# Gate and up products of an FP4 feed-forward regrouped into 512, 512 and 384 columns, with new instruction orders

## What is computed

```python
s = attn(xn)      # linear attention, 16 heads of 64, phi = elu + 1; + residual, LN; GELU FFN 256-1024-256; + residual, LN
gate = fp4_linear(xn, w_gate)               # 256 -> 704
y    = fp4_linear(xn, w_up)                 # 256 -> 704
g = silu(fp4_linear(silu(gate) * y, w_down))   # 704 -> 256
out = x + s * g
```

## Time and profile before

| | us |
|---|---|
| median of 3 runs | 1647.81 (1647.04 to 1648.1) |
| the profiled execution's own time | 1644.95 |
| its span in the trace | 1643.2 |
| PE busy, granted clock | 1604.9 (98%), 0.999 of full speed |
| DVE, ACT, POOL busy | 1280.4, 980.1, 783.3 |

### The profile page before, as it was taken

One profiled execution on the slowest core, in us unless ns is written; L12 is line 12 of the kernel. 1 busy time (PEld: TensorE's weight loads), 2 busy tenths in 40 slices (PEclk: granted clock), 3 DMA queues, 4 the chain that ended last, 5 costly groups with the idle time before them and its releaser, 6 DMA issues.

```text
span 1643.2 us, 30638 instructions
## 1 busy us (share of the span) xinstructions
PE 1604.9 (98%) x10977; PEld 1440.9 (88%) x10977; DVE 1280.4 (78%) x2485; ACT 980.1 (60%) x1770; POOL 783.3 (48%) x750
## 2 busy tenths in 40 slices
PE   7999999999899999999999999999999999999997
PEld 6878888888789998999999999989899989999897
DVE  6785664554788797888888887879788888878797
ACT  6665666655564747565665647474656656574743
POOL 4564543434242635444444536364455444363636
PEclk9999999999999999999999999999999999999999
DMA  7422323331501111133121112111121321111110
GB/s 227 136 84 86 104 78 106 103 109 57 186 15 53 52 53 52 53 111 91 47 68 53 52 53 107 53 52 53 52 60 61 104 87 58 53 52 53 52 53 26
DMA packets 92515, 123.46 MB, mean 75 GB/s; under 512 B 13503, under 2 KB 60747, under 8 KB 91342
## 3 DMA queue, kind: packets, MB, share of 16 engines
q1 hardware_dynamic: 92366, 121.51, 23.1%
HBM read 86.86 MB, written 34.62 MB: 74 GB/s over the span
## 4 chain that ended last, share of the span: by engine, by line
PE 68%; DVE 13%; DMA 7%; issue 5%; SPq 3%; ACT 3%; POOL 2%; DVEq 0%; POOLq 0%; ACTq 0%
PE QH L81 11%; PE QH L82 11%; PE QH L83 10%; PE AC L81 5%; PE AC L82 4%; PE AC L83 4%; DMA zb<-z_scratch 4%; PE GU L81 4%; PE GU L83 4%; PE GU L82 4%; DVE QH L1828 2%; PE TT L831 2%; DVE rl L1837 2%; SPq L408 2%; DMA z_scratch<-dn_s 1%
## 5 line engine op out<-in xcount | busy, mean ns | idle before, releaser
L2309 POOL TENSOR_TENSOR hb<-hb,rs_h 128x704 f32<-128x704 f32 x64 | 89.0, 1391 | 206.3 <-DVE rs_h L1680 206.3
L1248 ACT ACTIVATE hb<-GU 128x352 f32<-128x352 f32 x128 | 59.2, 463 | 214.3 <-PE GU L83 214.3
L1201 ACT ACTIVATE rh<-QH 128x512 fp32r<-128x512 f32 x256 | 151.2, 598 | 58.2 <-DVE QH L1828 53.2
L81 PE MATMUL GU<-wgh,xqh 128*128 128x352 f32 x512 | 169.8, 332 | 3.1 <-DVE hb L1673 3.1
L2315 POOL TENSOR_TENSOR hb<-hb,sn_h 128x64 f32<-128x64 f32 x64 | 18.8, 293 | 319.5 <-DVE hb L1685 319.5
L83 PE MATMUL GU<-wgh,xql 128*128 128x352 f32 x512 | 165.0, 322 | 0.0
L82 PE MATMUL GU<-wgl,xqh 128*128 128x352 f32 x512 | 164.9, 322 | 0.0
L1843 DVE TENSOR_TENSOR rl<-QH,rh 128x512 fp32r<-128x512 f32 x128 | 86.0, 682 | 85.8 <-ACT rh L1201 83.7
L81 PE MATMUL AC<-Mh,rh 128*128 128x256 f32 x512 | 145.9, 285 | 1.4 <-ACT rh L1201 0.6
L81 PE MATMUL AC<-w2h,rh 128*128 128x256 f32 x512 | 145.7, 285 | 0.0
L82 PE MATMUL AC<-Ml,rh 128*128 128x256 f32 x512 | 142.4, 278 | 0.0
(11 more groups left out here) (234 smaller groups left out, 5586.0 us busy)
## 6 DMA issues: line engine op xcount, KB each, us to landing
zb<-z_scratch SPq DMA_DIRECT2D x256, 128.0 KB, 3.0
xa<-in_L_attn_src SPq DMA_DIRECT2D x16, 512.0 KB, 4.2
xt_scratch<-xth SPq DMA_DIRECT2D x32, 256.0 KB, 2.7
xt_scratch<-xtl SPq DMA_DIRECT2D x32, 256.0 KB, 3.0
xb<-in_L_attn_src SPq DMA_DIRECT2D x16, 512.0 KB, 4.2
xnTh<-xt_scratch SPq DMA_DIRECT2D x32, 256.0 KB, 4.8
xnTl<-xt_scratch SPq DMA_DIRECT2D x32, 256.0 KB, 5.6
out<-x SPq DMA_DIRECT2D x15, 512.0 KB, 6.6
```

What stands on the lines that cost most here:

```text
L81: e.matmul(outp, lh, rh, start=start, stop=False, skip_group_check=check)
L1201: e.activation(RH[j % 4][:], src, ACT.Copy).then_inc(S[sem], 1)
L1248: e.activation(HB[i % 3][:, hf * HALF:(hf + 1) * HALF], gu_bank(i, hf)[:, 0:HALF], ACT.Tanh, scale=0.5).then_inc(S["th"], 1)
L2309: e.tensor_tensor(hb, hb, spread(rs_h[i % 2][:], 44), ALU.mult).then_inc(S["hin"], 1)
```

## The change

`gate_up(i, 0)` now makes 512 gate columns into the first bank of GU and 512 up columns into the second, 6 matmuls each, with a semaphore step after each part; `gate_up(i, 1)` makes the other 192 gate and 192 up columns together, as one run of 384 columns, 6 matmuls, into one bank (the first for even tiles, the second for odd). That is 18 matmuls a tile and 72 a group, in place of 24 and 96, over the same columns. The rows of the weights are loaded in the order that this needs. `gate_up(i, 0)` waits for each bank by itself; where the bank held a gate part only, it waits for hu, the first of DVE's two products. ACT and DVE have as many instructions as before, now of 512 and 192 columns.

Four dummy buffers move wgh, wgl and xqh, xql, Q32, eg, hb to 192 modulo 256 bytes and leave w2h, wdh and Mh at 224. All four engine lists are reordered.

```diff
-HALF = 352
+HEAD = 512
+SECTIONS = ((0, 512, 0, 0), (512, 512, 1, 0), (1024, 192, 0, 512), (1216, 192, 1, 512))
...
+GU_ORDER = ((0, 0), (0, 1), (1, 1), (1, 0), (2, 0), (2, 1), (3, 1), (3, 0))
+GU_ENDS = [sum(2 - hf for _, hf in GU_ORDER[:n + 1]) for n in range(8)]
...
+        sb("after_w2", [128, 56])
...
+        sb("after_wg", [128, 8])
...
+        sb("before_xq", [128, 8])
...
-        sb("before_m", [128, 32])
+        sb("before_m", [128, 24])
...
+        def gate_cols(i, hf):
+            return (GU[:, 0:512], HEAD) if hf == 0 else (GU[:, i % 2 * 512:i % 2 * 512 + 192], 704 - HEAD)
+        def up_cols(i, hf):
+            return GU[:, 512:1024] if hf == 0 else GU[:, i % 2 * 512 + 192:i % 2 * 512 + 384]
...
+                if hf:
+                    w.wait_ge(S["hu" if t % 2 == 0 else "hh"], n if t % 2 == 0 else n - 1)
+                    for kt in range(2):
+                        last = mm3(e, GU[:, t % 2 * 512:t % 2 * 512 + 384], xqh[:, kt, o:o + 128], xql[:, kt, o:o + 128],
+                                   wgh[:, kt, 1024:1408], wgl[:, kt, 1024:1408], kt == 0, kt == 1)
+                    last.then_inc(S["guG"], 1)
                 else:
+                    for up in range(2):
+                        if t % 2:
+                            w.wait_ge(S["hh"], n - 1 + up)
+                        else:
+                            w.wait_ge(S["hh" if up else "hu"], n)
+                        c = up * 512
+                        for kt in range(2):
+                            last = mm3(e, GU[:, c:c + 512], xqh[:, kt, o:o + 128], xql[:, kt, o:o + 128],
+                                       wgh[:, kt, c:c + 512], wgl[:, kt, c:c + 512], kt == 0, kt == 1)
+                        last.then_inc(S["guG"], 1)
```

More of the change, by code:

```diff
@@ L805, in gate_up @@
                 w.wait_ge(S["A_wTl"], 6)
[L806 to L809, removed]
-                else:
[L812 to L819, removed]
+                n = 8 * g + GU_ORDER.index((t, hf))
+                if hf:
[4 more added lines that the diff above has]
+                    last.then_inc(S["guG"], 1)
+                else:
+                    for up in range(2):
[8 more added lines that the diff above has]
+                        last.then_inc(S["guG"], 1)
             def turn_h(i, hf):
@@ L1026, in _ @@
+                turn_xq(g + 1, 0)
+                q_proj(g + 1, 6)
+                q_proj(g + 1, 7)
             f_step(NG - 2, 6)
             f_step(NG - 2, 7)
-            gate_up(NT - 3, 0)
+            den_sums(NG - 1)
+            gate_up(NT - 4, 0)
+            gate_up(NT - 4, 1)
+            gate_up(NT - 3, 1)
             down(NT - 6)
             turn_h(NT - 5, 0)
-            gate_up(NT - 3, 1)
-            turn_h(NT - 5, 1)
+            gate_up(NT - 3, 0)
             at_step(NG - 1, 0)
@@ L2034, in _ @@
             z_mul(0, 7)
[L2035 removed]
+            h_round(0)
             z_lo(0, 6)
             z_lo(0, 7)
[L2038 to L2039 removed]
+            gate_mul(1, 0)
+            xq_lo(0, 1)
             ln1_add(0, 0)
@@ L2107, in _ @@
                 z_mul(g, 3)
-                h_lo(d - 4, 1)
+                g_mul(c - 4)
                 z_lo(g, 2)
@@ L2112, in _ @@
                 z_mul(g, 5)
-                xq_lo(g, 1)
+                h_lo(d - 4, 1)
                 z_lo(g, 4)
@@ L2117, in _ @@
                 z_mul(g, 7)
-                gate_mul(b, 1)
+                h_round(a)
                 z_lo(g, 6)
                 z_lo(g, 7)
-                h_round(a)
-                g_mul(c - 4)
-                gate_mul(c, 1)
+                gate_mul(b, 0)
+                xq_lo(g, 1)
                 ln1_add(g, 0)
@@ L2174, in _ @@
                 q_elu(g + 1, 7)
-            x_round(NG - 1, 1)
-            gate_mul(NT - 4, 0)
-            den_inverse(NG - 1)
-            h_max(NT - 4)
-            h_scale(NT - 4)
-            ln_add("lnb", NG - 2, 0)
-            ln_add("lnb", NG - 2, 1)
-            ln_stats("lnb", NG - 2)
-            gate_mul(NT - 3, 0)
-            g_mul(NT - 6)
+                xq_lo(g + 1, 0)
+                ln_add("lnb", g, 0)
+                x_round(g + 1, 1)
+                den_inverse(g + 1)
+                ln_add("lnb", g, 1)
+                gate_mul(a + 4, 0)
+                ln_stats("lnb", g)
+            gate_mul(NT - 4, 1)
+            gate_mul(NT - 3, 1)
+            h_max(NT - 4)
             z_mul(NG - 1, 0)
@@ L2191, in _ @@
             z_mul(NG - 1, 3)
-            h_lo(NT - 5, 1)
+            g_mul(NT - 6)
             z_lo(NG - 1, 2)
@@ L2195, in _ @@
             z_mul(NG - 1, 4)
+            h_scale(NT - 4)
             z_mul(NG - 1, 5)
-            xq_lo(NG - 1, 1)
+            h_lo(NT - 5, 1)
             z_lo(NG - 1, 4)
```

609 lines of the change are left out of this document (332 added, 277 removed).

## The result

The changed kernel takes 1656.14 us in the median of 4 runs (1654.83 to 1656.72), the kernel before in the same comparison 1647.95 (1647.04 to 1648.32). The ratio is 1.0049 [1.0032, 1.0067], slower by 8.2 us. The forecast was 1642 with a range to 1655: the wrong sign, and outside. The profiled execution has a span of 1654.0 and an own time of 1655.8, 10.8 us more in span than the one before, which lay 2.9 us under its median.

What follows compares the result with a forecast made beforehand. It took PE's nearly gapless train of matmul calls, by product count and spacing, and its few stops as the bound. The terms -5.0 - 10.9 - 1.4 + 3.7 + 4.6 + 3.4 = -5.6 gave 1642 us, range 1630 to 1655.

Steps and rivals of the forecast that it cites:

- The stop that goes: PE's turn_h waiting behind h_lo, 8.7 us in 14 waits: expected to vanish, -10.9 us.
- D: In times such as D + 8.5, den_sums' end; as rival, 512-column products at the new place 8 ns slower, 1648, chance 0.05.
- at0's wait: PE's at0 right behind turn_h waits for z_lo0, 2.8 us in all; half taken as gone, -1.4 us.
- The products: Gate_up matmuls on PE: 0.227 us at 512 columns, 0.173 at 384, 0.078 less a tile, -5.0 us.
- The stops that come: Three new or longer waits on PE in the new order: +3.7, +4.6 and +3.4 us.
- (1): G(a,1) on PE waits for hu from G(a,0): 0.23 us, 16 times, +3.7 us.
- (2): turn_x1's second call on PE waits longer for ln1_norm: +0.3 us a group, 15 times, +4.6 us.
- (3): G(c,1) on PE waits for hu of (c,0), behind ln1_norm on DVE: 0.23 us, 15 times, +3.4 us.
- The other moves: Remaining reorderings, such as turn_xq, den_sums with f6 and f7 as cover, and the tail: costed at nothing.
- C: Rival: DVE's queue ahead of z_mul0, with den_inverse still late, makes it slower, 1657 or from 1651 up; chance 0.20.
- A: Rival: new order better balanced, the new stops hide and at0's whole wait goes, 1629; chance 0.15.
- B: Rival: stops only change places, products save 1 to 5 us, 1643 to 1647, say 1645.5; chance 0.24.

Runs made afterwards that it cites:

- e1: Changed kernel, but POOL's h_in(a) of a group's first tile waits until DVE has done h_lo(d',0); 1648.79 us, ratio 0.9996 to the kernel before.
- e6: Kernel before, with only h_scale(a) on VectorE and h_in(a + 4) on POOL moved to the changed kernel's places; 1664.04 us, ratio 1.008.
- e5: Changed kernel with h_lo(d - 4, 0) moved between z_mul(g, 0) and z_mul(g, 1) on VectorE; 1655.11 us, ratio 1.0032.
- e10: e9 with turn_h(d - 4, 0) also moved between G(a, 0) and G(a, 1) on PE; 1649.43 us, ratio 1.0003.
- e11: e3 with f_step(g - 1, 4) moved from ahead of q_proj(g, 4) to directly behind den_sums(g); 1658.39 us, ratio 1.0055.
- e3: Kernel before, products regrouped to 512, 512 and 384 columns, old orders and old buffer places; 1646.69 us, ratio 0.9979.
- e4: Whole changed kernel, but with the buffers at their old places; 1656.84 us, ratio 1.0046.
- e7: e3 with h_lo(d - 4, 0) moved between z_mul(g, 0) and z_mul(g, 1) on VectorE; 1651.16 us, ratio 1.0006.
- e9: e1 with turn_h(a, 1) moved between the two turn_x1 calls on PE; 1649.92 us, ratio 1.0006.
- e2: Kernel before, products regrouped to 512, 512 and 384 columns, old orders but new buffer places; 1647.91 us, ratio 0.9993.

## Why the prediction was wrong

**The stop that goes, -10.9: the step that failed.** The step said that h_lo would be 2.8 us less urgent and the stop would go "if the chain below holds". The chain held up to z_mul 0. It had den_inverse at D + 0.1 and z_mul 0 at D + 8.5; with D at 1120.61 they came at D + 0.2 and D + 8.3. Then the working took the pair z_mul 0 and 1 at the duration that it has alone, 1.3, and it took 2.47. The 12.6 us in 14 waits, each with 0.16 on top as in the forecast's own reading, cost 14.8 where 10.9 had been before: +3.9 in place of -10.9, which by itself turns -5.6 into +9. The working listed every instruction ahead of z_mul 0 on VectorE. It did not ask what the reciprocal, moved to directly ahead of z_mul 0, releases on POOL. e1 shows that this overlap is the cause of the loss, and e6 that it is enough by itself to make one. e5 adds that this stop could not have been had back at turn_h alone.

**Even without the collision the stop would have stayed in part.** e1 still has 4.5 us in 6 waits, and the DMA row in e10 says why. The path from den_sums over the denominators, the DMA and z_mul to h_lo and z_lo was already as long as PE's work beside it. More PE work behind turn_h's first half made h_lo less urgent against that half, but not against D, from which z_mul 0 and h_lo are counted. Before, PE was ready for turn_h(d',1) at D + 10.3 (1122.48 + 0.16); in the changed kernel it is ready at 1130.62 + 0.23, D + 10.2. The forecast's own numbers say the same: at0 at D + 10.6 less turn_h's 0.45 is D + 10.2, and h_lo's end is z_mul 0 at D + 8.5, the pair's 1.3 and h_lo's 0.4, again D + 10.2. That is a tie, so the -10.9 had no room behind it. This is a second error of the same step, and e1 fits it: without the overlap with z_mul 0 and 1 the kernel is back at the time before, and not 5.6 us under it. To get h_lo earlier, den_sums has to come earlier in PE's list, and e11 shows what stands against it.

**at0's wait, -1.4.** turn_h to at0 is 0.55 in starts, as it was: nothing gained. Off by 1.4.

**The products, -5.0.** Where no other width or transpose stands ahead the spacings are as forecast: G(d,0) of group 9 has 12 products in 2.72 us (1155.97 to 1158.69), 0.227 each, and the 384 settle at 0.173. But the first product behind a transpose or another width takes longer, 0.28 us at 384 columns (1123.67 to 1123.95 below), and the forecast had no such term. In G(a,0) and behind it group 9 has 512 columns at 0.230 (1122.10 to 1123.25 for five spacings), the 384 at 0.176 (1123.95 to 1125.71 for ten). That is 12 x 0.230 + 6 x 0.176 = 3.82 us a tile for 3.84 before, -1.5 us in all, below the 1.9 which the forecast had as the smaller end. The rows:

```profile
1122.10 0.40 PE L80 MATMUL GU<-wgh,xqh 128*128 128x512 f32 x1
...
1123.25 0.39 PE L82 MATMUL GU<-wgh,xql 128*128 128x512 f32 x1
1123.67 0.44 PE L80 MATMUL GU<-wgh,xqh 128*128 128x384 f32 x1
1123.95 0.33 PE L81 MATMUL GU<-wgl,xqh 128*128 128x384 f32 x1
...
1125.71 0.34 PE L82 MATMUL GU<-wgh,xql 128*128 128x384 f32 x1
```

The runs of e3 put the regrouping's whole worth in the old orders at 0.21% of 1649, 3.5 us; where the 2 us beyond the spacing come from was not followed up.

**The stops that come.** All three came, and a little smaller. (1) From the last 512 product at 1123.25 to the first 384 one at 1123.67 are 0.42, of which 0.23 is the spacing: 0.19, forecast 0.23. (2) turn_x1's second call in group 9 starts 1.01 behind the first, 0.57 more than the 0.44 without a stop, forecast 0.33 + 0.3. (3) G(c, 1) starts 0.60 behind that, 0.16 more than a turn, forecast 0.23. Together 0.19 x 16 + 0.24 x 15 + 0.16 x 15 = 9.0 us instead of 11.7. The rows for (2) and (3):

```profile
1149.39 0.60 PE L789 MATMUL QH<-ident,x 128*128 128x128 f32 x4
1150.40 0.66 PE L789 MATMUL QH<-ident,x 128*128 128x128 f32 x4 [0.41 <-DVE x L1847]
1151.00 0.45 PE L80 MATMUL GU<-wgh,xqh 128*128 128x384 f32 x1
```

**The other moves at nothing, and the places at nothing.** The tail is as it was, the places changed nothing in the changed kernel (e4), and no new wait of turn_xq or den_sums stands in the loop. But one term set at nothing was a gain. Before, den_sums stopped for Q in 14 of the 16 groups:

```profile
PE DN L723 <- DVE Q L1658: 2.5, 14, 0.2
```

With 0.16 on top of each that is 4.7 us. Afterwards this wait is gone from the list, and den_sums starts 0.21 behind the last product of f7 instead of 0.115, 1.4 us in all: 3.3 us gained by the better cover that the forecast itself named. The first den_sums is 2.3 us later, for which the last section has the likely reason.

**The rivals.** C had the sign and nearly the time (1657), and the right place, VectorE's queue between the reciprocal and the first at_step. Its mechanism, a den_inverse that is still late, did not occur, so its time was met by luck. A and B fell: the new orders don't balance better, and the stops did not merely change places. But B's rule, that a stop taken away here comes back there, is what e5, e7, e9, e10 and e11 each showed. D fell with e4; its 8 ns stand in none of the rows shown, and e2 and e3 have 1 ns between the places.

The sum in the profile: 14.8 for the step that failed, 3.5 for the products, 1.4 for at0, 2.3 ahead of the loop, less 2.7 for the three smaller stops and 3.3 for den_sums, is 16.0, where forecast (-5.6) and profile (+10.8) are 16.4 apart. Most terms are read from group 9 alone and taken times 15 or 16, so agreement this close is partly chance.

## What to carry to other kernels

When a step moves on one engine, list what its signal releases on the others, and look which instruction will run at that moment. Here a reciprocal of 0.4 us, moved past nothing that waited for it, put a 1.4 us GpSimd product onto a VectorE product that reads both its operands from SBUF. In a view of one line, the maximum beside the median finds this at once (735 ns in 128 before, 1882 after). It doesn't tell what this costs: h_scale and h_round had grown by more busy time, and e1 keeps that and is rid of the 8 us all the same. And where two waits hang on one path, taking one away is no gain: five runs here (e5, e7, e9, e10, e11) removed a stop of 3 to 12 us, and each found about its like elsewhere.

## What the hardware showed beside this

Held up by the other engine, the short side is hit hard: 0.20 us of work took 0.83 (e6), and an h_in of 1.39 took up to 1.91. Products with two SBUF operands are not the only ones: h_scale's first product (L1760, 128x44, one input) has a median of 0.27 us and a maximum of 1.53 in the changed kernel, and all 28 above 1 us ran beside a GpSimd product of 2.4 us.

TensorE's clock fell for a moment in a place where the code is the same in both kernels. The window from 47 to 57 us of the changed kernel (busy time of PE, PEld, DVE, ACT and POOL with counts, granted clock, DMA share, GB/s):

```profile
47.00:57.00 10.00, 10.00 (x34) 8.06 (x34) 4.82 (x6) 3.80 (x8) 1.88 (x4) 0.69 0.01 2
```

The same window of the kernel before:

```profile
47.00:57.00 10.00, 10.00 (x48) 8.30 (x49) 5.00 (x7) 5.40 (x11) 5.03 (x6) 1.00 0.08 12
```

A mean of 0.69 over 10 us is 6.2 us at 1.2 GHz instead of 2.4 and costs 3.1; that is about the 2.8 us by which the first q_proj is later (413.31 for 410.53), and more than the 2.3 ahead of the first den_sums. Just before it PE made 32 products of one column each (43.38 to 47.33), and it did so in e1 too. It isn't the change's doing: the stretch lies in a part that is alike in all kernels, and e1, the changed kernel but for one wait of POOL, has 1.00 in the window from 42 to 52, where the changed kernel has 0.72 and e3 0.83. A single profile can differ from its neighbour by 3 us in this way, which is also how far the profiled execution before (1644.95) lay under its median.
